# One decoder on one core: cross weights loaded over five steps, last passes of the four-bit network on GpSimd, the turn first in the cosine stage

## The chip, the cores and the metric

The kernel runs on one core of one Trainium2 chip. The metric is the device time of one execution in microseconds (us), lower is better. A core has five engines with instruction queues of their own: TensorE (PE, with its weight loads as PEld), VectorE (DVE), ScalarE (ACT), GpSimd (POOL) and SyncE (SP), which here only issues transfers. They wait for one another through semaphores.

## What is computed

Two decoder layers on x (16 batches, 128 rows, 128 columns) with a context (16, 128, 96). Every sublayer reads a layer norm of x and is added to x.

```python
x = x + self_attention(layernorm(x))            # 16 heads, causal
x = x + cross_attention(layernorm(x), ctx)      # 16 heads, logits clipped
x = x + experts(layernorm(x))                   # top 2 of 8
x = x + attention_over_batches(layernorm(x))    # 16 heads of 64
x = x + cosine(layernorm(x), ctx)               # dots / (|v| |t|), 64 wide
x = x + four_bit_network(layernorm(x))

def fp4_quant_dequant(x):                       # blocks of 16
    scale = max(max(abs(xb)) / 6, 1e-12)
    xn = xb / scale
    idx = searchsorted(MID, abs(xn))
    return GRID[idx] * sign(xn) * scale
def four_bit_network(x):                        # 128 -> 352 -> 128
    h = silu(fp4_linear(x, w_gate)) * fp4_linear(x, w_up)
    return fp4_linear(h, w_down)                # both operands quantised
```

## The kernel before

The kernel is a row of stages in order of time, each a block in which every engine has its own program. The order on an engine is the order in which the program lists its calls; nothing is rearranged later. x stays in SBUF (`M.x`). The change touches three stages.

**The first attentions** (`layer0_attentions`, 0 to about 305 us). Thirty-two steps t, 16 of self attention and 16 of cross attention, in a software pipeline. SyncE's program at step t first calls `spread_rows(t + 1)` (L298 for self attention: one row of the negated maxima, 8 KB, from `back` to `row`, whose SBUF is that of `over_xhi` and `over_xlo`), and then whatever else is to be moved: at t == 3 the whole of `M.cross_weights.load` (L146 to L156, 22 transfers, the last 16 of them eight numbers of a bias each), from t == 2 one transfer of zeros (`slots<-blank`, L319) a step, from t == 8 a part of the expert weights. TensorE's `scores(t)` waits for the row of its step before its four matmuls of L481; the exponentials (L568), and with them the rest of the step, follow. VectorE waits for the cross weights at t == 6 and copies them (`prepare`), and TensorE needs the copies at t == 12.

**The cosine stage** (`cosine_block`, 683 to 722 us). Eight steps u of two batches. On TensorE the loop body is `project(u + 1)` (L1650), `sums(u)` (L1656), `products(u)` (L1664), `turn(u + 2)` (L1643, two transposes of the normalised rows). ScalarE's is `biased(u + 1)`, `roots(u)`, `turned(u + 2)` (L1695, which brings the transposes to SBUF for `project(u + 2)`). GpSimd makes the limited scales (L1715), VectorE the cosines, the sum and its statistics.

**The four-bit network** (`mlp_block`, 722 us to the end). Eight steps u of two batches; a step works on the hidden values (128 x 704) of u and the input rows (128 x 256) of u + 2. All of it goes through `signed_step` on VectorE: k = 0 the maximum of a block (L1811), 1 its scale (L1813), 2 the inverse (L1815), 3 multiply (L1817), 4 and 5 round (L1819, L1821; k = 4 needs the magnitudes that ScalarE makes from the result of k = 3, L1947 and L1932), 6 multiply by the scale (L1822), hidden and rows in turn at each k. After k = 3 VectorE normalises the rows of u + 3 (L1978), at the step's end come `gate` (L1985, silu times up) and `back` (L2016, the sum into x). TensorE's step is `turn(u - 1)` (L1898), `front(u + 1)` (L1890, L1891), `down(u - 1)` (L1906), `turn_rows(u + 2)` (L1883). ScalarE's begins with `turned(u - 1)` (L1953). h, scale and xscale have one buffer each. GpSimd does nothing in this stage.

Of the kernel before, what the change touches and what calls it, by code (L numbers as in the profile page):

```python
# [126 lines left out]
class AttentionWeights:  # L127


    def __init__(self, sb, tag, cross):  # L130
# [12 lines left out]
        self.loads = 6 + H if cross else 7  # L143

    def load(self, eng, d, sem):
        eng.dma_start(self.wide_q[:, :].rearrange("p (g c) -> p g c", g=NG), d[self.tag + "_wq"]).then_inc(sem, 16)  # L146
        eng.dma_start(self.wide_k[:, :].rearrange("p (g c) -> p g c", g=NG), d[self.tag + "_wk"]).then_inc(sem, 16)
        eng.dma_start(self.wv[:, :], d[self.tag + "_wv"]).then_inc(sem, 16)
        if not self.cross:
            eng.dma_start(self.upperf[:, :], d["causal_upper"]).then_inc(sem, 16)  # L150
        eng.dma_start(self.sidef[:, :], d["three_rows" if self.cross else "causal_side"]).then_inc(sem, 16)
        eng.dma_start(self.wo[:, :], d[self.tag + "_wo"]).then_inc(sem, 16)
        eng.dma_start(self.bo[:, :], d[self.tag + "_bo"].broadcast_to([S, D])).then_inc(sem, 16)
        if self.cross:
            for h in range(H):
                eng.dma_start(self.bq[HD * h:HD * h + HD, :],  # L156
                              d[self.tag + "_bq"][h // 4, 32 * (h % 4):32 * (h % 4) + HD].rearrange("(e a) -> e a", a=1)).then_inc(sem, 16)
# [59 lines left out]
def layer0_attentions(nc, M, d):  # L217
# [11 lines left out]
    with ExitStack() as ctx:  # L229
# [45 lines left out]
        with nc.Block() as block:  # L275
# [3 lines left out]
            def _(sp):  # L279
# [24 lines left out]
                for t in range(FIRST, N):  # L304
# [6 lines left out]
                    if t == 3:  # L311
                        M.cross_weights.load(sp, d, s["cross_weights"])
# [334 lines left out]
            def _(dve):  # L647
# [91 lines left out]
                for t in range(FIRST, N + 1):  # L739
# [875 lines left out]
def cosine_block(nc, M, d):  # L1615
# [5 lines left out]
    with ExitStack() as ctx:  # L1621
# [13 lines left out]
        with nc.Block() as block:  # L1635

            @block.tensor
            def _(pe):
# [28 lines left out]
                for u in range(-2, N):  # L1667
                    if valid(u + 1, N):
                        project(u + 1, (u + 1) % 2)
# [3 lines left out]
                    if valid(u + 2, N):  # L1673
                        turn(u + 2, u % 2)
# [149 lines left out]

class Blocks:
# [13 lines left out]
def mlp_block(nc, M, d, out):  # L1839


    with ExitStack() as ctx:
        one = lambda n, shape: ctx.enter_context(nc.sbuf_tensor(f"mlp_{n}", shape, F32))
        two = lambda n, shape: [one(f"{n}{p}", shape) for p in range(2)]
        s = semaphores(nc, "mlp", """variance root rstd xn row_mag row_step row_ps xt hidden_ps silu h mag step
            clear ht_ps ht y_ps x_done out w_ps weights""")
        IP = 3 * 128
        xn, xq, xt = two("xn", [S, 2, D]), two("xq", [S, 2, D]), two("xt", [D, 2, S])
        xtmp, xscale, xinv = one("xtmp", [S, 2, D]), one("xscale", [S, 16, 1]), one("xinv", [S, 16, 1])
        hq, ht = two("hq", [S, 2, IP]), two("ht", [128, 2, 3, S])  # L1850
        h, g, tmp, scale, inv = one("h", [S, 2, I]), one("g", [S, 2, I]), one("tmp", [S, 2, I]), one("scale", [S, 44, 1]), one("inv", [S, 44, 1])
# [3 lines left out]
        split = lambda t: t.rearrange("p j (n k) -> p j n k", k=16)  # L1855

        with nc.Block() as block:
# [4 lines left out]
            def _(pe):  # L1862
# [16 lines left out]
                def turn_rows(u, p):  # L1879
                    wait(pe, s["row_step"], u, per=SIGNED_STEPS, plus=SIGNED_STEPS)  # L1880
# [12 lines left out]
                def turn(u, p):  # L1893
                    wait(pe, s["step"], u, per=SIGNED_STEPS, plus=SIGNED_STEPS)
# [26 lines left out]
                loop_staged(pe, N, step, ahead=3, first=3)  # L1921

            @block.scalar
            def _(act):
# [5 lines left out]
                def row_magnitudes(u, p):  # L1930
                    wait(act, s["row_step"], u, per=SIGNED_STEPS, plus=4)
# [13 lines left out]
                def magnitudes(u):  # L1945
                    wait(act, s["step"], u, per=SIGNED_STEPS, plus=4)
                    nc.scalar.activation(tmp[:, :, :], h[:, :, :], ACT.Abs, scale=ROUND).then_inc(s["mag"], 1)  # L1947
# [243 lines left out]
```

## Time and profile before

| | us |
|---|---|
| median of 3 runs | 806.65 (806.61 to 810.84) |
| the profiled execution | 807.06 |
| its span, first to last instruction | 805.3 |

| engine | busy us | share of the span |
|---|---|---|
| PE | 622.4 | 77% |
| DVE | 480.8 | 60% |
| PEld | 457.9 | 57% |
| ACT | 372.2 | 46% |
| POOL | 234.0 | 29% |

All rows come from the one profiled execution; 1.8 us lie around its span. A start is counted from the first instruction. Busy time of PE is the time in which a matmul was in flight. PEclk is the granted clock of TensorE: 1.00 is 2.4 GHz, 0.50 is 1.2 GHz. Instructions of one engine overlap by their latency, so what one takes of an engine is read from the start of the next, not from its duration. In brackets stands how long the engine was idle before a row, and who ended that.

### The profile page before, as it was taken

To read this page: it belongs to the slowest core of one execution; us is meant where nothing else is said; L and a number is where in the kernel's file an instruction comes from. 1 tells how busy PE (TensorE), PEld (TensorE's weight loads), DVE (VectorE), ACT (ScalarE), POOL (GpSimd) and SP (SyncE) were. 2 spreads that over 40 slices of the span, in tenths; PEclk is the share of its full clock that TensorE was granted. 3 is DMA by queue.
4 is the path that set the end of the run, shared out by engine and by line. 5 is a ranking of instruction groups with operands and counts; after the bars stand their busy time and mean duration, and the time that the engine had idled before them with its cause. 6 is when DMAs were issued, how large, how long until landed. Compare 5 with 4: busy or idle time off the path is not lost. (4 is left out here: it accounts for less than half of the span.)

```text
span 805.3 us, 16987 instructions
## 1 busy us (share of the span) xinstructions
PE 622.4 (77%) x6347; PEld 457.9 (57%) x6377; DVE 480.8 (60%) x1294; ACT 372.2 (46%) x801; POOL 234.0 (29%) x337
## 2 busy tenths in 40 slices
PE   4795999888999974356999913889999884875865
PEld 2453555555666543234998912667878773553554
DVE  2454554568878766742444336575756554458995
ACT  5472765768676722125444441634444423323432
POOL 3131222434444211761445560031313130230000
PEclk9898899999999995566999965999999997556797
DMA  3013243442212211115566441100000000000000
GB/s 98 2 31 90 56 105 104 108 113 71 56 38 73 68 39 48 51 55 172 202 211 213 170 105 31 53 2 2 2 2 2 2 2 1 1 0 1 13 15 26
DMA packets 53135, 48.95 MB, mean 61 GB/s; under 512 B 10331, under 2 KB 45645, under 8 KB 52797
## 3 DMA queue, kind: packets, MB, share of 16 engines
q1 hardware_dynamic: 47037, 41.09, 17.0%
q0 software_dynamic: 2496, 4.27, 1.7%
q10 hardware_dynamic: 3520, 2.50, 1.2%
q8 instruction: 51, 0.84, 0.4%
q14 instruction: 31, 0.25, 0.1%
HBM read 18.68 MB, written 15.54 MB: 42 GB/s over the span
## 5 line engine op out<-in xcount | busy, mean ns | idle before, releaser
L568 ACT ACTIVATE ptx<-bank 128x512 f32<-128x512 f32 x128 | 66.1, 602 | 99.4 <-PE bank L481 99.3
L1557 POOL COPY ptx<-over_pt 32x512 f32<-32x512 f32 x64 | 39.0, 610 | 138.6 <-DVE over_pt L1527 135.8
L1117 POOL DMA_INDIRECT results<-moe_y,moe_dest x46 | 45.3, 984 | 59.3 <-DVE moe_y L1254 51.4
L722 DVE SCALAR_TENSOR_TENSOR ptx<-ptx,bank 128x512 f32<-128x512 f32 x64 | 41.1, 684 | 25.2 <-PE bank L490 23.5
L707 DVE TENSOR_REDUCE l_m<-bank 128x4 f32<-128x512 f32 x64 | 40.9, 679 | 20.7 <-PE bank L465 20.7
L381 POOL TENSOR_TENSOR x<-x,l_back 128x128 f32<-128x128 f32 x32 | 14.6, 456 | 132.9 <-ACT l_back L581 121.8
L477 PE MATMUL bank<-ke 32*128 32x512 f32 x256 | 36.8, 641 | 19.4 <-issue 15.7
L1457 ACT ACTIVATE ke<-bank 64x512 f32<-64x512 f32 x64 | 38.0, 594 | 16.2 <-PE bank L1388 15.3
L681 DVE BATCH_NORM_STATS2 l_stats<-x 128x6 f32<-128x128 f32 x32 | 9.3, 291 | 54.6 <-POOL x L381 54.6
L707 DVE TENSOR_REDUCE l_m_raw<-bank 128x4 f32<-128x512 f32 x64 | 40.7, 674 | 0.1
L1112 POOL DMA_INDIRECT slots<-xs,moe_pos x32 | 32.3, 1010 | 28.6 <-DVE moe_pos L1197 18.6
L1431 PE MATMUL bank<-over_ot,over_wo 128*128 128x128 f32 x256 | 33.4, 285 | 6.1 <-DVE over_ot L1533 6.1
L1500 DVE COPY over_q<-bank 128x512 f32<-128x512 f32 x32 | 22.1, 691 | 24.7 <-PE bank L1388 24.7
L363 POOL TENSOR_TENSOR ke<-ke,heads 128x512 f32<-128x512 f32 x32 | 33.3, 1041 | 10.5 <-ACT ke L548 9.0
L508 PE MATMUL bank<-ptx,ke 128*32 128x128 f32 x1024 | 34.6, 276 | 2.3 <-DVE ptx L722 2.2
L1431 PEld LDWEIGHTS bank<-over_ot,over_wo 128*128 128x128 f32 x256 | 30.3, 194 | 8.1 <-DVE over_ot L1533 7.0
L508 PE MATMUL bank<-ptx,head_ones 128*32 128x128 f32 x1024 | 33.9, 273 | 0.0
L1040 ACT ACTIVATE moe_h<-bank,ptx 128x256 f32<-128x256 f32 x48 | 19.7, 471 | 28.6 <-PE bank L962 28.5
L727 DVE RECIPROCAL l_rden<-bank 128x128 f32<-128x128 f32 x32 | 30.4, 950 | 3.5 <-PE bank L508 3.5
L1421 PE MATMUL bank<-ptx,over_v 128*64 128x128 f32 x512 | 31.5, 276 | 0.0
L1421 PEld LDWEIGHTS bank<-ptx,over_v 128*64 128x64 f32 x512 | 27.6, 137 | 5.4 <-issue 4.8
L508 PEld LDWEIGHTS bank<-ptx,ke 128*32 128x32 f32 x1024 | 26.1, 109 | 7.1 <-issue 3.6
(344 smaller groups left out, 1636.0 us busy)
## 6 DMA issues: line engine op xcount, KB each, us to landing
slots<-blank SPq DMA_DIRECT2D x16, 528.0 KB, 4.7
ptx<-w SPq DMA_DIRECT2D x12, 578.0 KB
ke<-w SPq DMA_DIRECT2D x11, 578.0 KB, 3.3
w<-in_w SPq DMA_DIRECT2D x16, 256.0 KB
moe_xb<-slots SPq DMA_DIRECT2D x23, 132.0 KB
x<-in_x SPq DMA_DIRECT2D x4, 256.0 KB, 5.3
w<-results SPq DMA_DIRECT2D x4, 256.0 KB, 5.8
w<-results ACTq DMA_DIRECT2D x4, 256.0 KB, 5.6
```

The lines of the kernel that those rows point to most:

```text
L363: nc.gpsimd.tensor_tensor(kxx[t % 2][:, :, :], front[(t - 3) % 4][:, 1, :].rearrange("p (a k) -> p a k", a=1).broadcast_to([128, 4, S]), M ...
L477: nc.tensor.matmul(score_bank[g][:, :], k[r, :], qxx[t % 4][r, :, :].rearrange("p j q -> p (j q)"), start=True, stop=False, skip_group_che ...
L508: mm = nc.tensor.matmul(pv_bank[32 * g:32 * g + 32, part * S:(part + 1) * S], w, probs[t % 2][:, g, j * S:(j + 1) * S], start=(j == 0), st ...
L568: nc.scalar.activation(probs[t % 2][:, g, :], score_bank[g][:, :], ACT.Exp, scale=SCALE0).then_inc(s["probs"], 1)
L707: nc.vector.tensor_reduce(mx[:, 4 * g:4 * g + 4], top_bank[g][:, :].rearrange("p (j k) -> p j k", j=4), AX.X, ALU.max, negate=True).then_i ...
L722: nc.vector.scalar_tensor_tensor(probs[t % 2][:, g, :], probs[t % 2][:, g, :], 1.0, floor_bank[g][:, :], ALU.min, ALU.max).then_inc(s["cli ...
L1112: nc.gpsimd.indirect_dma_start(M.slots, bass.IndirectOffsetOnAxis(pos[:, k, 4 * q + j:4 * q + j + 1], 0), M.xs[:, 4 * q + j, :], None).the ...
L1117: nc.gpsimd.indirect_dma_start(M.results, bass.IndirectOffsetOnAxis(dest[j % 4][:, n:n + 1], 0), y[j % 4][:, n, :], None, bounds_check=2 * ...
L1421: mm = nc.tensor.matmul(o_bank[r // 4][j:j + 64, r % 4 * S:(r % 4 + 1) * S], v[t % 3][:, h // 8, h % 8 * HB:(h % 8 + 1) * HB], ptx[t % 2][ ...
L1431: mm = nc.tensor.matmul(y_bank[:, 0:S], wo[:, r, :], ot[t % 2][:, r, :], start=r == 0, stop=r == PAIR - 1)
L1457: nc.scalar.activation(ke[h, r, j, :], ring[at_block(t, r, 1) % 3][h, :], ACT.Copy).then_inc(s["ke"], 1)
L1557: nc.gpsimd.tensor_copy(ptx[t % 2][r, :, r], pt[t % 2][r, :, :]).then_inc(s["spread"], 1)
```

## The change

The cross weights go out in five parts, at t = 1 to 5, behind `spread_rows`; the 16 small transfers of the bias become four, two each in the last two parts; VectorE copies them at t == 7 instead of 6. In the cosine stage `turn(u + 2)` comes first in TensorE's step. In the four-bit network GpSimd normalises the rows and does the last pass (k = 6) of rows and hidden values (`last_step`, the same operation on the other engine); VectorE keeps k = 0 to 5; `back(u - 2)` comes after k = 1 of step u; h, scale and xscale are doubled; TensorE runs `front` before `turn`, ScalarE `turned` after the silus; the loops are written out (one hardware loop of two steps was there before).

```diff
-        self.loads = 6 + H if cross else 7
+        self.loads = 6 + NG if cross else 7
+    def load(self, eng, d, sem, part=None):
+        if part in (None, 0):
+            eng.dma_start(self.wide_q...
+            eng.dma_start(self.wide_k...
+        if part in (None, 1):
+            eng.dma_start(self.wv...
+            eng.dma_start(self.sidef...
+        if part in (None, 2):
+            eng.dma_start(self.wo...
+            eng.dma_start(self.bo...
+        if self.cross and part in (None, 3, 4):
+            for g in (0, 1) if part == 3 else (2, 3):
+                eng.dma_start(self.bq[32 * g:32 * g + 32, :],
+                              d[self.tag + "_bq"][g, :].rearrange("(j c a) -> j c a", c=32, a=1)[:, 0:HD, :]).then_inc(sem, 16)
...
-                    if t == 3:
-                        M.cross_weights.load(sp, d, s["cross_weights"])
+                    if 1 <= t < 6:
+                        M.cross_weights.load(sp, d, s["cross_weights"], t - 1)
...
-                    if t == 6:
+                    if t == 7:
                         dve.wait_ge(s["cross_weights"], 16 * M.cross_weights.loads)
...
                 for u in range(-2, N):
+                    if valid(u + 2, N):
+                        turn(u + 2, u % 2)
                     if valid(u + 1, N):
                         project(u + 1, (u + 1) % 2)
                     if valid(u, N):
                         sums(u, u % 2)
                         products(u, u % 2)
-                    if valid(u + 2, N):
-                        turn(u + 2, u % 2)
...
+def last_step(nc, c):
+    split = lambda t: t.rearrange("p (j n) k -> p j n k", j=c.rows)
+    return nc.gpsimd.tensor_tensor(c.q, split(c.a), split(c.scale).broadcast_to([c.p, c.rows, c.n // c.rows, 16]), ALU.mult)
...
                 def step(u, p):                       # TensorE
-                    if valid(u - 1, N):
-                        turn(u - 1, 1 - p)
                     if valid(u + 1, N):
                         front(u + 1, 1 - p)
                     if valid(u - 1, N):
+                        turn(u - 1, 1 - p)
                         down(u - 1, 1 - p)
...
                 def step(u, p):                       # ScalarE
-                    if valid(u - 1, N):
-                        turned(u - 1, 1 - p)
                     if valid(u, N):
-                        magnitudes(u)
+                        magnitudes(u, p)
                     if valid(u + 2, N):
                         row_magnitudes(u + 2, p)
                     if valid(u + 1, N):
                         front(u + 1, 1 - p)
+                    if valid(u - 1, N):
+                        turned(u - 1, 1 - p)
...
-                    for k in range(SIGNED_STEPS):
+                    for k in range(LAST):             # LAST = 6
...
-                        if k == 3 and valid(u + 3, N):
-                            normalise(u + 3, 1 - p)
+                        if k == 1 and valid(u - 2, N):
+                            back(u - 2)
...
+            @block.gpsimd
+            def _(pool):
+                def normalise(u, p):
+                    wait(pool, s["rows"], u, plus=-1)
...
+                def rows(u, p):
+                    wait(pool, s["row_step"], u, per=LAST, plus=LAST)
+                    wait(pool, s["row_ps"], u, plus=-1)
+                    last_step(nc, row_blocks[p]).then_inc(s["rows"], 1)
+                def hidden(u, p):
+                    wait(pool, s["step"], u, per=LAST, plus=LAST)
+                    wait(pool, s["ht_ps"], u, per=2, plus=-2)
+                    last_step(nc, hidden_blocks[p]).then_inc(s["hidden"], 1)
+                def step(u, p):
+                    if valid(u + 3, N):
+                        normalise(u + 3, 1 - p)
+                    if valid(u + 2, N):
+                        rows(u + 2, p)
+                    if valid(u, N):
+                        hidden(u, p)
```

## Rows read from the trace of the kernel before

**Rows 1.** The stretches of cosine stage and four-bit network: length, busy us, PEclk, DMA.
```profile
683.00:722.00 39.00, 29.65 (x96) 18.76 (x96) 19.31 (x81) 11.39 (x34) 12.08 (x16) 0.50 0.00 0
722.00:805.00 83.00, 54.82 (x234) 40.88 (x234) 68.47 (x156) 28.32 (x61) 0.00 (x0) 0.77 0.05 13
```

**Rows 2.** SyncE's timeline, 50 to 76 us: start, length of the issue, line, transfer.
```profile
50.61 0.50 SPq L298 DMA_DIRECT2D over_xlo<-l_back  x1
...
58.45 0.51 SPq L298 DMA_DIRECT2D over_xhi<-l_back  x1
...
61.40 6.86 SPq L151 DMA_DIRECT2D cross_sidef<-in_three_rows  x1
...
69.62 5.66 SPq L156 DMA_DIRECT2D cross_bq<-in_cross_bq  x16
...
75.83 0.53 SPq L298 DMA_DIRECT2D over_xlo<-l_back  x1
```

**Rows 3.** TensorE's timeline: the matmuls that need the row.
```profile
55.44 1.20 PE L481 MATMUL bank<-over_xlo,self_side 128*128 128x512 f32 x4
...
79.42 2.08 PE L481 MATMUL bank<-over_xlo,self_side 128*128 128x512 f32 x4 [8.18 <-DMA over_xlo<-l_back]
```

**Rows 4.** Busy time from one issue of L298 to the next, columns as in group 1.
```profile
82.73:92.81 10.08, 9.36 (x107) 5.41 (x111) 4.30 (x10) 7.16 (x15) 3.71 (x4) 0.89 0.20 56
...
116.85:124.67 7.82, 7.33 (x101) 4.61 (x105) 4.30 (x10) 6.97 (x15) 1.92 (x3) 1.00 0.48 128
```

**Rows 5.** Timeline of one step of the cosine stage.
```profile
699.33 0.69 PE L1643 MATMUL bank<-ident,cos_xn 128*128 128x128 f32 x2
...
700.06 0.38 ACT L1695 ACTIVATE cos_xt<-bank 128x256 f32<-128x256 f32 x1 [1.51 <-PE bank L1643]
...
700.49 1.11 PE L1650 MATMUL bank<-cos_xt,cos_wv 128*64 128x256 f32 x2 [0.47 <-ACT cos_xt L1695]
...
703.54 0.69 PE L1643 MATMUL bank<-ident,cos_xn 128*128 128x128 f32 x2
```

**Rows 6.** The same timeline at the stage's end.
```profile
713.11 1.11 PE L1650 MATMUL bank<-cos_xt,cos_wv 128*64 128x256 f32 x2 [0.47 <-ACT cos_xt L1695]
...
718.31 1.61 POOL L1715 TENSOR_SCALAR cos_m<-cos_inv 128x128 f32<-128x128 f32 x2 [0.83 <-DVE cos_inv L1735]
```

**Rows 7.** Timeline of one step of the four-bit network.
```profile
750.89 0.88 DVE L1811 TENSOR_REDUCE mlp_scale<-mlp_h 128x44 f32<-128x704 f32 x1
...
753.62 0.79 ACT L1947 ACTIVATE mlp_tmp<-mlp_h 128x704 f32<-128x704 f32 x1 [2.10 <-DVE mlp_h L1817]
753.84 0.60 DVE L1978 TENSOR_SCALAR mlp_xn<-x,mv_b,rstd 128x128 f32<-128x128 f32 x2
...
754.51 0.89 DVE L1819 SCALAR_TENSOR_TENSOR mlp_h<-mlp_tmp,mlp_h 128x704 f32<-128x704 f32 x1
...
756.79 0.89 DVE L1822 TENSOR_TENSOR mlp_hq<-mlp_h,mlp_scale 128x704 f32<-128x704 f32 x1
...
759.12 0.88 DVE L1811 TENSOR_REDUCE mlp_scale<-mlp_h 128x44 f32<-128x704 f32 x1
```

**Rows 8.** GpSimd's groups by shape: count, busy us, mean ns, idle before.
```profile
L363 POOL TENSOR_TENSOR ke<-ke,heads 128x512 f32<-128x512 f32 x32 | 33.3, 1041 | 10.5 <-ACT ke L548 9.0 <-POOL l_lt_parts L376 0.4
...
L381 POOL TENSOR_TENSOR x<-x,l_back 128x128 f32<-128x128 f32 x32 | 14.6, 456 | 132.9 <-ACT l_back L581 121.8 <-issue 11.1
L353 POOL TENSOR_SCALAR l_xn<-x,l_mv,l_rstd 128x128 f32<-128x128 f32 x16 | 12.8, 797 | 0.0
```

**Rows 9.** Timeline at 480 us: the same normalisation on VectorE beside GpSimd.
```profile
480.04 1.38 DVE L1279 TENSOR_SCALAR moe_xn<-x,mv_b,rstd 128x128 f32<-128x128 f32 x1
480.07 1.26 POOL L1125 TENSOR_TENSOR w<-w 128x512 f32<-128x512 f32 x1 [0.79 <-DMA w<-results]
```

**Rows 10.** TensorE's timeline in the network at the lower clock.
```profile
743.58 1.38 PE L1890 MATMUL bank<-gate_w,mlp_xt 128*128 128x352 f32 x2
744.76 1.38 PE L1891 MATMUL bank<-up_w,mlp_xt 128*128 128x352 f32 x2
```

More of the change, by code:

```diff
@@ L1844, in mlp_block @@
         two = lambda n, shape: [one(f"{n}{p}", shape) for p in range(2)]
-        s = semaphores(nc, "mlp", """variance root rstd xn row_mag row_step row_ps xt hidden_ps silu h mag step
-            clear ht_ps ht y_ps x_done out w_ps weights""")
+        s = semaphores(nc, "mlp", """variance root rstd xn row_mag row_step rows row_ps xt hidden_ps silu h mag step
+            hidden clear ht_ps ht y_ps x_done out w_ps weights""")
         IP = 3 * 128
         xn, xq, xt = two("xn", [S, 2, D]), two("xq", [S, 2, D]), two("xt", [D, 2, S])
-        xtmp, xscale, xinv = one("xtmp", [S, 2, D]), one("xscale", [S, 16, 1]), one("xinv", [S, 16, 1])
+        xtmp, xscale, xinv = one("xtmp", [S, 2, D]), two("xscale", [S, 16, 1]), one("xinv", [S, 16, 1])
         hq, ht = two("hq", [S, 2, IP]), two("ht", [128, 2, 3, S])
-        h, g, tmp, scale, inv = one("h", [S, 2, I]), one("g", [S, 2, I]), one("tmp", [S, 2, I]), one("scale", [S, 44, 1]), one("inv", [S, 44, 1])
+        h, scale = two("h", [S, 2, I]), two("scale", [S, 44, 1])
+        g, tmp, inv = one("g", [S, 2, I]), one("tmp", [S, 2, I]), one("inv", [S, 44, 1])
+        LAST = SIGNED_STEPS - 1
         gate_bank, up_bank, ht_bank, y_bank, row_bank = M.bank[0:2], M.bank[2:4], M.bank[4:6], M.bank[6], M.bank[7]
@@ L1855, in mlp_block @@
         split = lambda t: t.rearrange("p j (n k) -> p j n k", k=16)
+        hidden_blocks = [Blocks(S, 44, 2, cut(h[p]), None, scale[p][:, :, :], inv[:, :, :], cut(tmp), split(hq[p][:, :, 0:I])) for p in range(2)]
+        row_blocks = [Blocks(S, 16, 2, cut(xn[p]), None, xscale[p][:, :, :], xinv[:, :, :], cut(xtmp), split(xq[p][:, :, :])) for p in range(2)]
         with nc.Block() as block:
@@ L1879, in turn_rows @@
                 def turn_rows(u, p):
-                    wait(pe, s["row_step"], u, per=SIGNED_STEPS, plus=SIGNED_STEPS)
+                    wait(pe, s["rows"], u, plus=1)
                     wait(pe, s["xt"], u)
@@ L1893, in turn @@
                 def turn(u, p):
-                    wait(pe, s["step"], u, per=SIGNED_STEPS, plus=SIGNED_STEPS)
+                    wait(pe, s["hidden"], u, plus=1)
                     wait(pe, s["ht"], u, per=2)
@@ L1920, in step @@
                         turn_rows(u + 2, p)
-                loop_staged(pe, N, step, ahead=3, first=3)
+                for u in range(-3, N + 1):
+                    step(u, u % 2)
             @block.scalar
@@ L1943, in front, with magnitudes @@
                         nc.scalar.activation(g[:, j, :], gate_bank[j][:, 0:I], ACT.Silu).then_inc(s["silu"], 1)
[L1945 to L1947 removed]
+                def magnitudes(u, p):
+                    wait(act, s["step"], u, per=LAST, plus=4)
+                    nc.scalar.activation(tmp[:, :, :], h[p][:, :, :], ACT.Abs, scale=ROUND).then_inc(s["mag"], 1)
                 def turned(u, p):
@@ L1963, in step @@
                         front(u + 1, 1 - p)
+                    if valid(u - 1, N):
+                        turned(u - 1, 1 - p)
                     if valid(u + 2, N):
                         turned_rows(u + 2, p)
-                loop_staged(act, N, step, ahead=3, first=3)
+                for u in range(-3, N + 1):
+                    step(u, u % 2)
             @block.vector
```

63 lines of the change are left out of this document (29 added, 34 removed).

## Prediction, made before the changed kernel was run

> **What bounds the kernel now.** The page's busy shares are means over stages with different limits (PE 77%, DVE 60%), so I read each of the three touched stages by itself: the busy times of the stretch, then the timeline of one regular step, and in it the one instruction that everything else waits for.
>
> The first attentions have a period that TensorE sets: two issues of the row transfer lie 7.84 us apart [rows 2], TensorE is busy for 7.33 of 7.82 us [rows 4]. One step falls out. SyncE issues the row of a step at 58.45 and the next only at 75.83 [rows 2]: between them stand the 22 transfers of the cross weights, of which one issue alone held SyncE for 6.86 us and the 16 small ones 5.66 us. TensorE sat idle for 8.18 us for that row [rows 3], and until the row issued at 92.81 the clock was 0.89 [rows 4], that is 1.2 GHz for a part, after TensorE had been idle. This wait is on the path that sets the end: the steps are strictly in line.
>
> In the cosine stage (39 us) the clock is 0.50 throughout and PE is busy for 29.65 us, DVE for 19.31 us [rows 1]. A step takes 4.21 us (699.33 to 703.54), and TensorE is at rest in it once: from the transposes to `project`, while ScalarE moves the transposes to SBUF [rows 5]. TensorE bounds the stage, with one handshake in each step.
>
> In the four-bit network VectorE is busy for 68.47 of 83 us [rows 1], and a step takes 8.23 us (750.89 to 759.12) [rows 7]. VectorE bounds it, and TensorE, with clock 0.77 [rows 1], waits.
>
> **Part 1, cross weights over five steps.** Removed: the burst behind the row of t = 3. From 58.45 to 92.81 lie three steps, 34.36 us [rows 2, 4]. Three regular ones take 3 x 7.83 = 23.5 us. If no row comes late, the whole difference goes: 10.9 us, idle time and slow clock together. Moved: each part is issued right behind the row of its step, where SyncE then rests until the next row. Two issues of about 0.6 us and the zeros of 0.6 us take 2 us of 7.8. What the cover must hold: a row is issued at 50.61 and used at 55.44 [rows 2, 3], so a part of the step before may delay its landing by some 2.5 us before TensorE waits. The doubtful part is the first, the two wide weights: they stood ahead of the issue that took 6.86 us [rows 2]. In its new place it has 7.8 us until the next row is issued. The evidence for "no wait" is a step in which SyncE issued a 256 KB part of the expert weights, the zeros and the row, with the DMA engines busy 0.48, and which took 7.82 us [rows 4]. Bounds: the wait recurs once and costs 6.86 - 2.5 = 4.4 us, or not at all; I take nothing, by the nearer row. The copies on VectorE move by a step and TensorE needs them five steps later: nothing. Sum: -10.9 (ends -6.5 and -11).
>
> **Part 2, turn first.** Between the second transpose and `project` TensorE loses the transposes' latency and ScalarE's copy. The two transposes hold TensorE for about 0.48 us: 0.69 in flight, and where matmuls follow without a gap the next starts 0.2 us before the end of those ahead (743.58 + 1.38 against 744.76) [rows 10]. So of 700.49 - 699.33 = 1.16 us [rows 5] 0.68 are waiting. In the new order the copy of u + 2 has `products` (1.13 us) and the next `turn` as cover: it starts after `roots`, some 0.2 us after `sums` has ended, and takes 0.38 us. The wait goes entirely and a step becomes 3.53 us. What is late next is the loop of VectorE and GpSimd: scale, limit (1.61 us for the pair [rows 6]), cosine, next inverse, 2.44 us in the last two steps, where nothing else held it. It doesn't bind. In the head the first steps gain nothing, since ScalarE's order (`biased` before `turned`) holds them; from `project(2)` to `project(6)` five waits go, 3.3 us, and before `project(7)`, at 713.11 now [rows 6], there is a sixth, together with the transposes themselves, which already lie a step earlier: 1.16 us. The tail behind it is the same. Sum: 3.3 + 1.1 = -4.4 us (ends -3.3 and, if the clock rises, -9).
>
> **Part 3, last passes and normalisation on GpSimd.** VectorE loses in a step the two last passes, 757.93 - 756.79 = 1.14 us to the gate behind them, and two normalisations, 0.60 us [rows 7]. The second brings nothing: k = 4 at 754.51 waits for ScalarE's magnitudes (753.62 + 0.79) [rows 7], and with the normalisations gone VectorE stands still in their place. So a step is 8.23 - 1.14 = 7.09 us if GpSimd disturbs nothing.
>
> GpSimd's prices: normalisation 2 x 0.80 us (same form, L353). The last pass has no row. L381 and L363 give 0.456 us at 128 and 1.041 at 512 columns, 1.52 ns a column, so 0.65 us for 256 and 1.33 for 704; in L1125, with two full operands, 512 columns took 1.26 [rows 9], which gives 1.66 for 704. I take 0.65 and 1.4; with 1.6, 3.7 us of a step [rows 8]. GpSimd has room.
>
> The Trainium skill gives for two inputs about 2.6 cycles a column at 1.2 GHz (GPSIMD Engine Reference, Performance versus the Vector engine); an estimate by it is 1.5 us for the hidden pass, and no row here has that pattern.
>
> But the two engines hinder each other. A normalisation of 0.34 us on VectorE took 1.38 us while GpSimd's operation ran, and ended 0.05 us after it (480.04 + 1.38, 480.07 + 1.26) [rows 9]. VectorE's k = 1, 3, 4, 5 are of that kind or read two tensors of SBUF. The Trainium skill says so in general: VectorE's second SBUF port pair is shared with GpSimd, taken for a whole instruction, and an operation with two SBUF inputs needs it too (SBUF — State Buffer, Who interferes with whom). The trace agrees for the normalisation. In a step, counted from the gate: GpSimd's rows 0.1 to 0.8, hidden 0.8 to 2.3, beside gate and maxima, which are free of it; k = 1, due at 2.1, waits until 2.3; then two normalisations to about 4.1, while k = 3 is due at 3.1. If k = 3 gets in between the two, the step is 0.45 us longer, if it waits for both 1.3 us: 7.55 to 8.4 us. I take 7.9.
>
> Sum of the stage: five steps with a normalisation, now 8.0 to 8.6 us each, 2.5 us less in all; step 5 (no normalisation) 0.8; step 6 (no rows) 0.95; in the last step the pass is on the path and costs 1.4 and a hand-over instead of 0.9, and `back` has moved before it: +1.0; at the start normalisation (1.6 for 0.6) and first pass of the rows are on the path, and k = 1 meets GpSimd's second normalisation: +2.0. The new order on TensorE costs nothing at full clock: the rows come 1 us later, `front` takes 2.4 us, gate(u + 1) is due 5 us after. At 1.2 GHz `front` takes 4.7 us (0.59 a matmul [rows 10]) and the gate waits about 1 us; a clock of 0.77 [rows 1] means 46% of the stage; I put 0.6 us. Together 2.5 + 0.8 + 0.95 - 1.0 - 2.0 - 0.6: -0.6 us (ends -6 and +5).
>
> **Sum.** 807.06 - 10.9 - 4.4 - 0.6 = 791.2 us against the profiled execution. The median is 0.4 us below that execution, so 791.0 is my figure (790.8, rounded).
>
> **The rivals.** (a) The cosine stage, denser, is granted the higher clock. It has had 0.50 for the whole of it [rows 1] with PE at 76%, and goes to 85%. A step is then bound by the 2.44 us loop: 5 x 1.0 less, 786. (b) GpSimd and VectorE don't disturb each other in the network: 5 x 0.8 + 1 less there, 786. (c) GpSimd wins each tie: 5 x 0.5 more and more at the start, 795. (d) A part still makes a row late: 4.4 more, 795.4. (e) The clock is 0.50 through the whole network. TensorE needs there (0.21 us for 128 columns, by [rows 10]) 4.7 + 12 x 0.21 + 6 x 0.21 + 0.48 = 9.0 us a step and, with the order front, turn, down, rows, two hand-overs to ScalarE of 0.7 us: 10.4, 2.2 above 8.23, over 7 steps 15 us, and all is lost: 807, no change. It decides once more than half of the steps run so; against it, TensorE's rests get shorter. (f) Slower: the last pass on GpSimd, blocks of 16 with a held scale, is no match for the rows I took. All that VectorE does with the shared port (3.7 us a step) stands in line with it. To eat up the 15.3 us of parts 1 and 2 and 4 more, a step must reach 10.6 us, so GpSimd 6.9, so the hidden pass 4.6 us, three times the dearer row. At 5.5 us: 8 x 3.3 - 15.3, 818 us. (g) Part 1 doesn't do what it says, because the row waits for something else than SyncE's queue: against it speak the gap from 58.45 to 75.83 in that queue and 79.42 behind it [rows 2, 3].
>
> **How the numbers follow.** Forecast 0.60; (a) 0.12; (b) 0.09; (c) 0.07; (d) 0.06; (e) and (g) 0.03; (f) 0.03. The range takes in (a) to (d) with the bounds of part 3: 784.0 to 797.5; left out are (e), (f), (g) and combinations at both ends. 0.5%, 4 us, is about what a measurement of this kernel can tell from no change: faster by more 0.94, within 0.03, slower 0.03.
>
> **What would show it.** Part 1: seven issues of L298 in a row 7.8 us apart, no wait of L481 for a transfer, clock 1.00 from 58 to 100 us; wrong if one L298 comes over 2 us late. Part 2: `project` in step with the transposes, period 3.5 us, stage 4.4 us shorter. Part 3: k = 3 to 5 with a few instances far above 0.89 us, each ending with a GpSimd operation; period 7.5 to 8.4 us; last pass of the hidden values 1.3 to 1.7 us. What would make the prediction wrong above all: the lock in the network and the clock, together 6 us either way.

## The result, and the profile after

| | before | after |
|---|---|---|
| median, us | 807.57 (806.61 to 810.84, 4 runs) | 787.75 (785.98 to 788.09, 4 runs) |
| the profiled execution, its span | 807.06, 805.3 | 788.09, 786.3 |
| first attentions, to us | 306.2 | 296.3 |
| experts | 173.8 | 176.3 |
| attention over batches | 203.7 | 203.6 |
| cosine stage | 38.39 | 34.53 |
| four-bit network | 83.13 | 75.67 |

The ratio after to before is 0.9746 (95%: 0.9721 to 0.9771): faster, by 19.8 us. The stages are cut at the same points of the program in every kernel. Their differences, -9.94 + 2.42 - 0.16 - 3.86 - 7.46 = -19.0 us, make up the difference between the two spans.

From the page of the changed kernel, the span and the busy time of each engine (share of the span, instructions):

```profile
span 786.3 us, 16978 instructions
PE 620.1 (79%) x6347; PEld 453.4 (58%) x6377; DVE 467.1 (59%) x1262; ACT 370.0 (47%) x801; POOL 265.1 (34%) x369
```

Thirty-one us of work came to GpSimd and 13.7 left VectorE; TensorE does the same. Busy time of three stretches: a step of the first attentions, cosine stage, four-bit network (columns as in [rows 1]):

```profile
74.26:82.08 7.82, 7.33 (x101) 4.61 (x105) 4.30 (x10) 6.96 (x15) 3.65 (x4) 1.00 0.27 72
676.08:710.61 34.53, 29.14 (x97) 18.84 (x98) 18.53 (x80) 10.33 (x32) 12.32 (x16) 0.50 0.00 0
710.61:786.30 75.69, 50.84 (x234) 35.75 (x234) 55.50 (x124) 27.20 (x61) 30.99 (x32) 0.85 0.05 15
```

The network's clock went from 0.77 [rows 1] to 0.85, that of the cosine stage stayed at 0.50, though PE is now in flight for 29.14 of 34.53 us.

**First attentions.** SyncE's timeline around what was the burst (start, length of the issue), and TensorE's use of the row:

```profile
50.68 0.51 SPq L303 DMA_DIRECT2D over_xlo<-l_back  x1
51.72 1.30 SPq L155 DMA_DIRECT2D cross_sidef<-in_three_rows  x1
58.52 0.51 SPq L303 DMA_DIRECT2D over_xhi<-l_back  x1
66.35 0.51 SPq L303 DMA_DIRECT2D over_xlo<-l_back  x1
...
63.34 1.20 PE L486 MATMUL bank<-over_xhi,self_side 128*128 128x512 f32 x4
```

The rows are issued 7.84 and 7.83 us apart, where before 17.38 us passed between 58.45 and 75.83 [rows 2]. The same transfer behind the wide weights now holds SyncE for 1.30 us, not 6.86, and TensorE no longer waits for a row [rows 3].

**Cosine stage.** One step on TensorE and ScalarE (start, busy time, in square brackets the idle time before):

```profile
691.20 1.12 PE L1655 MATMUL bank<-cos_xt,cos_wv 128*64 128x256 f32 x2
...
693.37 0.38 ACT L1700 ACTIVATE cos_xt<-bank 128x256 f32<-128x256 f32 x1
694.25 0.69 PE L1648 MATMUL bank<-ident,cos_xn 128*128 128x128 f32 x2
694.87 0.29 PEld L1655 LDWEIGHTS bank<-cos_xt,cos_wv 128*64 128x64 f32 x2 [0.33 <-issue]
694.87 1.12 PE L1655 MATMUL bank<-cos_xt,cos_wv 128*64 128x256 f32 x2
```

`project` no longer names ScalarE as what it waited for [rows 5]: ScalarE's copy ended at 693.75. A step takes 3.67 us (691.20 to 694.87) instead of 4.21.

**Four-bit network.** One step on VectorE and GpSimd:

```profile
751.46 0.62 POOL L1834 TENSOR_TENSOR mlp_xq<-mlp_xn,mlp_xscale 128x256 f32<-128x256 f32 x1 [2.88 <-DVE mlp_xn L1826]
752.04 1.38 POOL L1834 TENSOR_TENSOR mlp_hq<-mlp_h,mlp_scale 128x704 f32<-128x704 f32 x1
752.27 0.89 DVE L1816 TENSOR_REDUCE mlp_scale<-mlp_h 128x44 f32<-128x704 f32 x1
...
753.40 0.18 DVE L1818 TENSOR_SCALAR mlp_scale<-mlp_scale 128x44 f32<-128x44 f32 x1
753.41 2.38 POOL L2040 TENSOR_SCALAR mlp_xn<-x,mv_b,rstd 128x128 f32<-128x128 f32 x2
753.52 0.17 DVE L1818 TENSOR_SCALAR mlp_xscale<-mlp_xscale 128x16 f32<-128x16 f32 x1
...
754.39 0.89 DVE L1822 SCALAR_TENSOR_TENSOR mlp_h<-mlp_inv,mlp_h 128x704 f32<-128x704 f32 x1
755.20 0.51 DVE L1822 SCALAR_TENSOR_TENSOR mlp_xn<-mlp_xinv,mlp_xn 128x256 f32<-128x256 f32 x1
756.21 0.89 DVE L1824 SCALAR_TENSOR_TENSOR mlp_h<-mlp_tmp,mlp_h 128x704 f32<-128x704 f32 x1 [0.50 <-ACT mlp_tmp L1963]
...
759.47 0.89 DVE L1816 TENSOR_REDUCE mlp_scale<-mlp_h 128x44 f32<-128x704 f32 x1
```

A step is 7.20 us (752.27 to 759.47), was 8.23 [rows 7]; the seven between the first and the last maximum of the hidden values take 49.12 us, before 56.99. The rows show how tight it is. GpSimd's hidden pass ends at 753.42, and VectorE's k = 1 starts at 753.40, 1.13 us after the maximum as it did before the change: nothing held it up. At k = 3 it is GpSimd that is held up: its two normalisations take 2.38 us, the second of them 1.52 (754.27 to 755.78), while VectorE's two k = 3 take 0.89 and 0.51 us.

GpSimd's groups in the network (count, busy us, mean ns, idle before):

```profile
L2040 POOL TENSOR_SCALAR mlp_xn<-x,mv_b,rstd 128x128 f32<-128x128 f32 x16 | 15.3, 961 | 3.3 <-DVE rstd L213 3.1
L1834 POOL TENSOR_TENSOR mlp_hq<-mlp_h,mlp_scale 128x704 f32<-128x704 f32 x8 | 11.1, 1384 | 9.4 <-DVE mlp_h L1826 9.4
L1834 POOL TENSOR_TENSOR mlp_xq<-mlp_xn,mlp_xscale 128x256 f32<-128x256 f32 x8 | 5.0, 620 | 27.9 <-DVE mlp_xn L1826 27.9
```

The start and the end of the stage, where both new pieces stand on the path:

```profile
711.47 3.12 POOL L2040 TENSOR_SCALAR mlp_xn<-x,mv_b,rstd 128x128 f32<-128x128 f32 x4 [3.08 <-DVE rstd L213]
713.15 0.42 DVE L1816 TENSOR_REDUCE mlp_xscale<-mlp_xn 128x16 f32<-128x256 f32 x1 [1.79 <-POOL mlp_xn L2040]
...
777.63 0.89 DVE L1826 SCALAR_TENSOR_TENSOR mlp_h<-mlp_tmp,mlp_h 128x704 f32<-128x704 f32 x1
778.60 1.38 POOL L1834 TENSOR_TENSOR mlp_hq<-mlp_h,mlp_scale 128x704 f32<-128x704 f32 x1 [4.95 <-DVE mlp_h L1826]
```

### The profile page after: what moved, and what is told of

The parts are those of the page before. It is cut to its first block and busy times, and to the rows that moved or that the text cites. A ratio compares the mean times of both kernels' runs of the same rounds, so it can differ in the third digit from the quotient of the medians.

```text
span 786.3 us, 16978 instructions
## 1 busy us (share of the span) xinstructions
PE 620.1 (79%) x6347; PEld 453.4 (58%) x6377; DVE 467.1 (59%) x1262; ACT 370.0 (47%) x801; POOL 265.1 (34%) x369
## 5 line engine op out<-in xcount | busy, mean ns | idle before, releaser
L482 PE MATMUL bank<-ke 32*128 32x512 f32 x256 | 37.4, 651 | 19.1 <-issue 15.5
```

The lines of the kernel that those rows point to most:

```text
L482: nc.tensor.matmul(score_bank[g][:, :], k[r, :], qxx[t % 4][r, :, :].rearrange("p j q -> p (j q)"), start=True, stop=False, skip_group_che ...
```

## The experiments

They ran on three chips: p1 to p3 and v_norm_on_dve on one, after_again, w, x and y on a second, q and z on a third. On them the kernel before takes 796 to 805 us (medians 799.2, 798.8 and 798.8) and the expert stage 166 to 168, so each ratio is against the kernel before on the same chip, and stages are compared among these runs. Stage lengths in us, from one profiled execution each; where no ratio stands, the kernel was executed only once:

| | attentions to | experts | cosine | network | ratio to before (95%) |
|---|---|---|---|---|---|
| p1_weights | 298.5 | 167.4 | 38.43 | 82.46 | 0.9874 (0.9814 to 0.9934) |
| p2_turn | 305.4 | 165.9 | 34.52 | 82.56 | 0.9945 (0.9918 to 0.9972) |
| p3_network | 306.3 | 165.6 | 38.39 | 75.64 | 0.9909 (0.9885 to 0.9934) |
| after_again | 297.2 | 165.7 | 34.53 | 75.47 | 0.9775 (0.9725 to 0.9826) |
| v_norm_on_dve | 298.6 | 168.1 | 34.54 | 74.96 | 0.9729 (0.9668 to 0.9790) |
| w_tail_on_dve | 295.8 | 167.3 | 34.53 | 74.65 | 0.9747 (0.9716 to 0.9778) |
| x_pass_twice | 296.7 | 166.7 | 34.53 | 85.92 | |
| y_old_order | 297.9 | 167.9 | 34.54 | 77.07 | |
| q_four_bias | 304.2 | 166.9 | 38.38 | 82.91 | |
| q_96_rows | 296.3 | 165.9 | 38.43 | 83.05 | |
| q_spread_sixteen | 297.3 | 165.7 | 34.52 | 76.16 | |
| z_both | 297.9 | 165.9 | 34.52 | 74.28 | 0.9713 (0.9690 to 0.9736) |

### The three parts alone

Each is the kernel before with one part of the diff shown ahead of the prediction: p1_weights the five parts of `load`, p2_turn the place of `turn`, p3_network the rest.

> The kernel before with the cross weights alone spread over five steps. Theory (each part of the change acts in its own stage and they add up): SyncE's row transfers come 7.8 us apart from the second on, no matmul of the causal side waits for a transfer, the first attentions end 9.9 us earlier, as in the changed kernel; about 797 us if nothing behind them changes, 799 if the expert stage is 2.4 us longer again as it was there (176.3 us from its first normalised row to the first of the batch attention, against 173.8 before). Rival (the expert stage loses time because the attention ends differently): 176 us there in this run, and 174 in the runs that leave the weights alone.

> The kernel before with the turn first in the cosine stage alone. Theory: a step of the stage takes 3.66 instead of 4.21 us and the stage 3.9 us less, as in the changed kernel; clock still 0.50 there; about 803 us. Rival (the gain needs the other parts, through the clock): under 2 us.

> The kernel before with the changes in the four-bit network alone. Theory: the stage takes 7.5 us less (75.7 instead of 83.2), 7.2 us a regular step; about 799.5 us. Rival (the network's gain in the changed kernel was partly the luck of the clock's phase): 3 to 5 us less, with stretches at 0.50 in which TensorE holds the gate up.

Measured: 790.73, 795.31 and 791.93 us. Each alone gains less than 2%, but no interval takes in 1, and each acts in its own stage and leaves the other two changed stages as they are. The product of the three ratios, 0.9874 x 0.9945 x 0.9909 = 0.9730, agrees within the intervals with those of the whole (0.9746, and after_again 0.9775, whose own interval reaches to 0.9826): nothing large is won or lost by having them together. The network alone gives as much as in the whole (75.64 against 75.47 to 75.67), so its gain doesn't come from what stands before it; against the old network on the same chip (82.46 and 82.56) it is 6.9 us. In p1_weights the two steps around the burst take 7.90 and 7.83 us (from ScalarE's first exponential of a step to that of the next); in p2_turn, where nothing of them changed, 16.41 and 9.75.

### What in the burst costs the time

Rival explanations of the 6.86 us issue and what follows: the number of transfers, or the two transfers of 97 rows (wide_k and wv). q_four_bias is the kernel before with 4 bias transfers instead of 16, all still at t == 3:

```diff
-            for h in range(H):
-                eng.dma_start(self.bq[HD * h:HD * h + HD, :], ...)
+            for g in range(NG):
+                eng.dma_start(self.bq[32 * g:32 * g + 32, :], ...)
```

> The kernel before, cross weights still all at t = 3, but the bias in 4 transfers instead of 16. Theory (SyncE's queue is one line, and each issue stands in it): the 16 issues of 5.66 us become 4 of about 3 us together, the row comes 2.5 to 4 us earlier, the two steps around it take 23 instead of 26.5 us, a little more back if the lower clock is not reached. Rival (the row waits for the landing of what is ahead, not for the issues): no change in the steps.

q_96_rows is the kernel before with the two transfers each cut into 96 rows and one:

```diff
-        eng.dma_start(self.wide_k[:, :]..., d[self.tag + "_wk"])
-        eng.dma_start(self.wv[:, :], d[self.tag + "_wv"])
+        cuts = (0, 96, C + 1) if self.cross else (0, D)
+        for lo, hi in zip(cuts, cuts[1:]):
+            eng.dma_start(self.wide_k[lo:hi, :]..., d[self.tag + "_wk"][lo:hi, :, :])
+            eng.dma_start(self.wv[lo:hi, :], d[self.tag + "_wv"][lo:hi, :])
```

> The kernel before, all at t = 3, but the two weights of 97 rows loaded as 96 rows and one row. Theory (97 rows can't be dealt out over the 16 DMA engines, so one of them carries all rows of both, the queue of this one runs full and holds the issue of the next transfer for 6.86 us): that issue takes under 1.5 us, the row comes 5 to 7 us earlier, the two steps take 20 to 21 instead of 26.5 us. Rival (the queue is full of everything that stands in it, the zeros above all): the long issue stays within 1 us of 6.9 us, perhaps at another transfer.

SyncE's timeline of q_four_bias:

```profile
61.59 7.14 SPq L151 DMA_DIRECT2D cross_sidef<-in_three_rows  x1
...
70.09 2.88 SPq L156 DMA_DIRECT2D cross_bq<-in_cross_bq  x4
...
73.57 0.57 SPq L298 DMA_DIRECT2D over_xlo<-l_back  x1
```

And of q_96_rows:

```profile
61.08 0.37 SPq L153 DMA_DIRECT2D cross_sidef<-in_three_rows  x1
...
62.44 6.00 SPq L158 DMA_DIRECT2D cross_bq<-in_cross_bq  x16
...
69.00 0.53 SPq L300 DMA_DIRECT2D over_xlo<-l_back  x1
```

With four bias transfers the issue behind wv still takes 7.14 us, the next row goes out at 73.57, and the two steps take 13.53 + 9.80 us, 3.2 less than before (16.45 + 10.08). Cut at 96 rows the same issue takes 0.37 us, the row goes out at 69.00, and the two steps take 9.28 + 7.83: 9.4 of the 10.8 us come back with all 24 transfers still at one place. The stage ends at 296.3 us, as early as with the spreading (295.8 to 298.6). It was the 97 rows. The zeros, which the rival expectation named, are moved as before in this kernel. The times of single executions say less: 790.19 us beside 796.38 for the kernel before points the same way, 797.36 for q_four_bias doesn't show its 3 us, which are less than executions of equal code differ by.

Why they are slow is in the windows of the kernel before (the last two numbers: DMA engines' mean busy share, GB/s), two us each behind the issue of wv:

```profile
62.00:64.00 2.00, 1.80 (x11) 0.98 (x12) 1.55 (x5) 0.13 (x1) 0.30 (x1) 1.00 0.06 24
64.00:66.00 2.00, 1.95 (x14) 1.34 (x13) 0.00 (x0) 2.00 (x5) 0.16 (x1) 1.00 0.07 26
```

And in those of q_96_rows:

```profile
60.00:62.00 2.00, 1.64 (x61) 1.37 (x52) 2.00 (x6) 0.00 (x0) 0.00 (x0) 1.00 0.81 249
62.00:64.00 2.00, 1.93 (x12) 1.06 (x13) 1.43 (x4) 0.26 (x1) 0.43 (x1) 1.00 0.67 89
```

A share of 0.06 to 0.07 is one engine of sixteen (1/16 = 0.0625), at 24 to 26 GB/s; in the trace the packets of 2 KB leave one by one, 0.08 us apart. The two transfers, 242.5 KB together, need some 10 us so (an estimate from that rate). With 96 rows 0.81 of the engines move 249 GB/s. The Trainium skill says the same in general (DMA: Bandwidth & Descriptors, Why a DMA increments its semaphore by 16 and not by 1): a transfer is spread over the largest number up to 16 that divides the outer dimension on both of its sides, here the rows, and 97 is divided only by 1. The timelines show besides that the transfer queued behind them, itself one of 128 rows, holds SyncE for most of the time for which that one engine works.

### The normalisations back on VectorE, and the changed kernel once more

```diff
+                        if k == 3 and valid(u + 3, N):     # VectorE
+                            normalise(u + 3, 1 - p)
...
-                    if valid(u + 3, N):                    # GpSimd
-                        normalise(u + 3, 1 - p)
```

> The changed kernel with the normalisation of the rows left on VectorE, behind k = 3 as before. Theory of the prediction (k = 4 waits for ScalarE's magnitudes, so the 0.60 us of the two normalisations lie in a gap): a regular step stays within 0.1 us of 7.2; the start gets 0.9 us shorter, because VectorE takes 0.6 for GpSimd's 1.6 us; 0.5 to 1.5 us less than the changed kernel. Rival (the lock: VectorE's two normalisations are delayed by GpSimd, or the gap is no longer there): 0.6 us more in each of five steps, 2 to 3 us more than the changed kernel.

> The changed kernel once more, beside the next ones on the same chip. Every theory: 0.972 to 0.977 of the kernel before; network 75.7 us, cosine stage 34.5 us.

VectorE's timeline in v_norm_on_dve:

```profile
747.36 0.89 DVE L1822 SCALAR_TENSOR_TENSOR mlp_h<-mlp_inv,mlp_h 128x704 f32<-128x704 f32 x1
...
748.50 0.60 DVE L1995 TENSOR_SCALAR mlp_xn<-x,mv_b,rstd 128x128 f32<-128x128 f32 x2
749.18 0.89 DVE L1824 SCALAR_TENSOR_TENSOR mlp_h<-mlp_tmp,mlp_h 128x704 f32<-128x704 f32 x1
```

The two normalisations fit into the gap in front of k = 4: from k = 3 to k = 4 pass 1.82 us, with them and without them (754.39 to 756.21 in the changed kernel), and a regular step is 7.20 us in both. So this half of part 3 brings nothing. At the start of the stage it costs 0.7 us: VectorE's first `gate` comes 9.94 us into the stage, and 10.64 in all six kernels with the normalisations on GpSimd. Up to the first maximum it is 12.64 us instead of 13.21 and 13.34, but p3_network, with the normalisations on GpSimd, has 12.57: there the clock rises to 1.00 at 10.4 us of the stage, in the changed kernel at 12.0, and the second `gate`, which waits for what ScalarE makes of TensorE's result, is earlier by 0.78 us. 779.56 us and 779.83, on two chips: no difference that these runs can tell.

### The last of the hidden passes back on VectorE

```diff
+                    if u == N - 1:                         # VectorE, after k = 5
...
+                        signed_step(nc, LAST, hidden_blocks[p]).then_inc(s["hidden"], 1)
...
-                    if valid(u, N):                        # GpSimd
+                    if valid(u, N - 1):
                         hidden(u, p)
```

It stands on v_norm_on_dve.

> The changed kernel with the normalisation back on VectorE and the last pass of the hidden values of the last step on VectorE too, where nothing else is left to do. Theory (GpSimd is dearer wherever nothing covers it: 1.6 us for 0.6 at the start, 1.38 and a hand-over for 0.9 at the end): start 0.7 us and end 0.5 us shorter than in the changed kernel, regular steps the same; 1.2 us less. Rival (VectorE is again the longer path as soon as it gets work back): steps longer by 0.3 us and more, no gain.

778.74 us, stage 74.65; its end (from the last maximum of hidden values on) is 13.04 us against 13.21. A pass of 1.38 us gives way to one of 0.9 us, and in this profiled execution a third of that arrives; the ratios of v_norm_on_dve, w_tail_on_dve and after_again can't be told apart.

### The hidden pass twice

```diff
                 def hidden(u, p):
                     ...
+                    last_step(nc, hidden_blocks[p]).then_inc(s["twice"], 1)
+                    wait(pool, s["twice"], u, plus=1)
                     last_step(nc, hidden_blocks[p]).then_inc(s["hidden"], 1)
```

The same product is written twice.

> The changed kernel with GpSimd's last pass of the hidden values done twice (the second waits for the first), 1.4 us more of GpSimd in a step, 5.3 of 7.2. Theory A (the two engines exclude each other on SBUF, and the changed kernel escapes it because GpSimd's hidden pass ends when VectorE's k = 1 is due): the second pass now lies over k = 1, and normalisations over k = 3 to 5; k = 1 and some of k = 3 to 5 take up to 1.4 us longer, ending with a GpSimd operation; steps of 8.0 to 9.0 us. Theory B (VectorE is the stronger one, GpSimd alone is held up): steps stay at 7.2 to 7.4 us, GpSimd's operations get longer. Theory C (no exclusion worth speaking of): neither changes.

GpSimd and VectorE in one step:

```profile
745.69 2.85 POOL L1834 TENSOR_TENSOR mlp_hq<-mlp_h,mlp_scale 128x704 f32<-128x704 f32 x2
745.93 0.89 DVE L1816 TENSOR_REDUCE mlp_scale<-mlp_h 128x44 f32<-128x704 f32 x1
...
747.17 1.40 DVE L1818 TENSOR_SCALAR mlp_xscale<-mlp_xscale 128x16 f32<-128x16 f32 x1
748.53 2.53 POOL L2040 TENSOR_SCALAR mlp_xn<-x,mv_b,rstd 128x128 f32<-128x128 f32 x2
...
754.40 0.89 DVE L1816 TENSOR_REDUCE mlp_scale<-mlp_h 128x44 f32<-128x704 f32 x1
```

VectorE's k = 1 of the rows, 16 columns, takes 1.40 us instead of 0.17 and ends at 748.57, 0.03 us after GpSimd's second pass (745.69 + 2.85 = 748.54). The maxima before it, 0.89 us, are untouched. The step is 8.47 us (745.93 to 754.40), 1.3 more than 7.20; the kernel's one execution took 788.69 us. So the exclusion that the prediction took from [rows 9] is there, at full price, once the GpSimd pass reaches k = 1. In the changed kernel it isn't reached: k = 1 starts 0.02 us before the end of the pass, and its two instructions take their usual 0.18 and 0.17 us. The Trainium skill's rule is in line with it (SBUF — State Buffer, Who interferes with whom): a VectorE operation in a two-port mode or with two SBUF inputs contends with GpSimd, the one that issues first keeps the shared ports for its whole instruction, and a maximum (`tensor_reduce`) never contends on trn2.

### The old order on TensorE and ScalarE

```diff
                 def step(u, p):                       # TensorE
+                    if valid(u - 1, N):
+                        turn(u - 1, 1 - p)
                     if valid(u + 1, N):
                         front(u + 1, 1 - p)
                     if valid(u - 1, N):
-                        turn(u - 1, 1 - p)
                         down(u - 1, 1 - p)
                 def step(u, p):                       # ScalarE
+                    if valid(u - 1, N):
+                        turned(u - 1, 1 - p)
                     if valid(u, N):
                         magnitudes(u, p)
...
-                    if valid(u - 1, N):
-                        turned(u - 1, 1 - p)
```

> The changed kernel with the old order on TensorE (turn before front) and ScalarE (turned before the magnitudes). Theory: the turned values of u - 1 now come from GpSimd 2.3 us into a step, so ScalarE, which waits for them first, starts the magnitudes about 1 us late and k = 4 with them: steps of 8.0 to 8.3 us, the whole gain of the moved passes gone. Rival (the order costs nothing at full clock, as the prediction has it for TensorE): 7.2 us.

ScalarE's timeline:

```profile
753.95 0.87 ACT L1970 ACTIVATE mlp_ht<-bank 128x384 f32<-128x384 f32 x2 [1.13 <-PE bank L1914]
755.14 0.79 ACT L1964 ACTIVATE mlp_tmp<-mlp_h 128x704 f32<-128x704 f32 x1 [0.32 <-DVE mlp_h L1822]
```

I expected 8.0 to 8.3 us a step, because `turned` would hold up the magnitudes. That fell: the regular step is 7.20 us again. The transposed values are moved at 753.95 and done at 754.82, the magnitudes are due only at 755.14. The new order costs nothing and brings nothing in the steady steps. The stage is 1.6 us longer (77.07 against 75.47), 1.5 of it behind the last maximum of hidden values (14.64 us against 13.12). But the granted clock of the last 7 us is 0.50 here and 0.91 in after_again (y_old_order first; columns as in [rows 1]):

```profile
773.40:780.40 7.00, 3.72 (x16) 3.05 (x14) 0.42 (x1) 0.98 (x2) 0.00 (x0) 0.50 0.12 37
770.70:777.70 7.00, 3.46 (x22) 2.76 (x21) 0.84 (x2) 0.87 (x2) 0.81 (x1) 0.91 0.12 37
```

And two kernels with the new order, p3_network and q_spread_sixteen, have 0.74 there and need 14.12 and 14.30 us. So the end of the stage goes with the clock, and the order isn't shown to cost anything.

### Sixteen bias transfers, spread, and both together

q_spread_sixteen is the changed kernel with 8 + 8 small bias transfers in the last two parts instead of 2 + 2; z_both is w_tail_on_dve with the same.

```diff
-            for g in (0, 1) if part == 3 else (2, 3):
+            for h in range(8) if part == 3 else range(8, 16):
```

> The changed kernel with the bias in 16 transfers again, eight each in the last two parts. Theory: eight issues of 0.34 us fit behind a row (2.8 of 7.8 us), so the five steps stay at 7.8 us and the splitting alone, not the smaller number, brought the 10.8 us. For what was given back behind them (step 17 at 10.7 to 11.6 us in three runs with the weights spread, 9.6 to 10.0 in three without; the first expert result 1.4 to 2 us later): if it hangs on the number of transfers that went through the queue before, step 17 falls to 10.0 or less here; if on the weights being out of the way earlier, it stays above 10.5.

> The changed kernel with the normalisation and the last step's hidden pass back on VectorE (as in the run that had both) and with the bias in 16 transfers, eight in each of the last two parts. Theory: the step behind the first context loads takes 9.6 to 10.0 us instead of 10.5 to 11.6, the network 74.7 us; 0.970 to 0.974 of the kernel before, 1 to 2 us less than with either alone. Rival (that step moved by chance in the runs so far): 10.5 us and more, and no more gain than from the network.

With all sixteen bias transfers spread, the steps stay at 7.83 to 7.90 us: it is the spreading, not the smaller number, that keeps the rows on time. The second question was where the changed kernel gives back a part of its gain. The first step of cross attention waits for the context. TensorE's waits there (us in all, times, longest), changed kernel and then q_spread_sixteen:

```profile
PE bank L435 <- DMA l_cb<-in_ctx: 2.3, 1, 2.3
```

```profile
PE bank L435 <- DMA l_cb<-in_ctx: 1.2, 1, 1.2
```

That step takes 10.27 to 11.59 us in all eight kernels with four bias transfers, q_four_bias among them, and 9.59 to 10.01 in the six with sixteen, spread or not. So it goes with the bias transfers, sixteen of eight numbers or four of 32 rows, and not with when they are issued; whether by their number or their form, and by what way, isn't shown. But what is won there is lost again: q_spread_sixteen ends its attentions at 297.3 us and after_again at 297.2. The loss is at the end: from ScalarE's first exponential of the last step to the end of the attentions pass 13.79 us in q_spread_sixteen and 13.85 in z_both, 12.50 or 12.51 in the twelve others. In these two the granted clock falls to 0.50 between 4 and 5 us behind that exponential, in the others 8 us or more; why it falls earlier isn't shown.

q_spread_sixteen takes 778.23 us. z_both takes 776.87 us, 0.9713 of before, the smallest ratio of all. The changed kernel has 0.9775 on a second chip and 0.9746 in the result, and the intervals overlap (0.9725 to 0.9736 with after_again's), so z_both isn't shown to be faster. By the profile the difference is in the network (74.28 against 75.47 to 75.67) and mostly w_tail_on_dve's gain.

## Why the prediction was right, and what in it was wrong

The median of 787.75 us lies in the range of 784.0 to 797.5, 3.3 below the forecast. Against its own span the forecast was -15.9 us, measured -19.0. The sum is nearer than its terms, and that is luck, as the end of this section shows.

**Part 1, forecast -10.9.** In the steps it is exact: 16.45 + 10.08 us became 7.90 + 7.84, which is 10.8 less; every row is issued 7.8 us apart and the clock from 58 to 100 us is 1.00. Of its two bounds, that the wait recurs once or not at all, the second came out, as forecast. What failed is the tacit step behind it, that what the path gains at 75 us arrives at the end. At the stage's end 9.9 us are left, behind experts and batches 7.7. On the other chips: attentions end at 305.4 and 306.3 us without the spreading (p2_turn, p3_network), at 297.5 in the mean of the eight kernels with it (295.8 to 298.6), so 8.4 of 10.6 us arrive. Of the missing 2.2 us, 0.9 is the first cross step and 0.3 the lower clock at the end in two of the eight. 1.0 us lies ahead of step 3, where kernels of one kind differ by as much among themselves (55.5 to 56.7 us without the spreading, 55.5 to 57.7 with it). The experts take 165.6 and 165.9 us without, 166.8 in the mean with it (165.7 to 168.1), and on the first chip 2.4 us more with it; this isn't explained.

What held the one issue for 6.86 us, which the prediction left open, are the 97-row transfers on one DMA engine.

**Part 2, forecast -4.4.** Measured -3.9: the mechanism is right, the wait for ScalarE is gone, and the clock stayed at 0.50 against rival (a). Mis-sized is the occupation of TensorE by the two transposes, 0.48 us by a subtraction taken from matmuls of 352 columns: `project` starts 0.62 us after them (694.25 to 694.87), with an idle 0.33 us of "issue" before its weights. So a step is 3.67 us, not 3.53: five of them gave 0.54 us each, 2.7 instead of 3.3, while the last `project` gave its 1.16 us as forecast. That is the missing 0.5.

**Part 3, forecast -0.6.** Measured -7.5: this term was wrong. Its sum doesn't even follow from its own step: the five steps took 8.02 to 8.58 us, 41.3 in all, and five of 7.9 are 1.8 us less, not 2.5. Four sizes in it:
- The exclusion. Forecast 7.9 us a step, measured 7.20. The prediction had 7.09 for no disturbance at all, and the 0.11 us between aren't one: the maximum now follows the second half of `gate` directly and starts when its result is there, 0.54 us after its start (751.73, 752.27), where before the change `back` followed it after 0.43 us (750.13, 750.56). Over the seven steps -7.9 us instead of -4.25. For k = 1 I had the right operations and a loss of 0.2 us (pass until 2.3, k = 1 due at 2.1); it was 0, since the pass ends 0.02 us after k = 1 is due. The larger share, 0.45 to 1.3 us, was k = 3, where I had VectorE as the one that waits; it was GpSimd, whose second normalisation has room to wait in. It starts 0.12 us before VectorE's k = 3 (754.27, 754.39), so what decides who waits isn't shown. The gap before k = 4, which the prediction itself had found, is there (0.50 us, for ScalarE).
- The start: +0.85 instead of +2.0. Up to the first `gate` it is +1.05 (10.64 us for 9.59). The normalisations took 0.78 to 0.80 us each, and k = 1, which met one of them, took 0.24 us instead of 0.17. The rest goes with when the clock rises.
- The end: -0.45 instead of +1.0. The pass on the path costs 1.38 as forecast, but the end varies with the clock, 13.12 to 14.30 us in kernels with the same network and 13.65 before, so this term isn't settled by one execution.
- The clock: 0.6 us for waits of the gate. It rose from 0.77 to 0.85 instead: 1.00 was granted from 26 to 66 us of the stage, and the regular steps there, 7.19 to 7.36 us, show at most 0.2 us of such a wait.

Together 3.6 + 1.2 + 1.4 + 0.6 = 6.8 us. The prices of the single GpSimd operations were right: 1.384 us (taken 1.4), 0.620 (0.65), 0.78 to 0.80 undisturbed (0.80). An estimate by the Trainium skill's 2.6 cycles a column was 1.5 us (GPSIMD Engine Reference, Performance versus the Vector engine); the measured 1.384 us lies a little below it, and the row of this trace was the better guide.

In its network this was rival (b), no disturbance, to which I gave 0.09 and a gain of 5 us over the forecast; it came to 6.9. It met a loss of 3.2 us behind part 1 and 0.5 in part 2. So the number was right by terms that balance: 15.9 + 6.9 - 3.2 - 0.5 = 19.1, the measured 19.0 up to rounding.

## What to carry over

When two engines exclude each other, the price is not the sum of what could collide but a question of tenths of a microsecond: lay both engines' operations of one step side by side on a time axis, ask for each pair what it costs if the one waits and if the other does, and give a range with both ends instead of a middle value. Half of a change can be worthless while the whole is fast: moving work out of a gap that stands in front of another wait brings nothing. And before a burst of transfers is spread over time, look at the row count of each: here one cut at 96 rows gave nearly all that the spreading gave.

## What the runs showed of the hardware

- A transfer of 97 rows (194 and 48.5 KB) was carried by one DMA engine at 24 to 26 GB/s, and the two together held the issue behind them for 6.83 to 7.20 us in four kernels; cut into 96 + 1 rows 249 GB/s and 0.37 us.
- Sixteen transfers of a few bytes held SyncE for 5.65 to 6.00 us, about 0.36 each; four of 32 rows 2.88 us, 0.72 each: four times fewer transfers halve the time.
- A 16-column operation of VectorE waited for a whole GpSimd pass, 1.40 instead of 0.17 us. The other way, GpSimd's second normalisation took 1.52 us instead of 0.8 (2.38 for the pair) beside VectorE's operations on two tensors, which lost at most 0.1 us.
- GpSimd's product with a scale held for 16 columns: 1.384 us at 704 columns, 0.620 at 256, so 1.7 ns a column.
- In the cosine stage TensorE had matmuls in flight for 84% of 34.5 us, and the granted clock was 0.50 from its beginning to its end.
